# Row 0's attention maxima moved into the mixer's last stretch, and the late rows' norm and queries spread over rows 3 to 10

## The chip, the cores and the metric

One core of one Trainium2 chip. The metric is the device time of one execution in microseconds (us). The core has five engines with queues of their own, tied by semaphores: TensorE (PE in the profile, its weight loads PEld), VectorE (DVE), ScalarE (ACT), GpSimd (POOL) and SyncE (SP, which issues most transfers).

## The reference

Three layers, each added to its input and layer-normalised: a state-space mixer, a grouped-query attention over a given context, and a mixture of experts. The change touches the seam between the first two and the attention. The attention is:

```
x = layernorm(x + mixer(x));  x = layernorm(x + attention(x, ctx, ctx));  x = layernorm(x + experts(x))
attention(q, k, v): 32 query heads, 8 key heads of width 8, 16 rows of 128 tokens
    scores = q k^T / sqrt(8);  out = softmax(scores) v
```

## The kernel before

The kernel is two blocks, one after the other; every engine has a program of its own in each, and the second block starts when all engines have ended the first.

**The mixer** (`mixer`, from L84) runs 32 steps, a step for each of 8 head groups and 4 blocks of tokens (of 4 rows each). A step projects, takes scores of pairs of heads (`scores`, L822), weighs them by decays (`weigh`, L613, on VectorE), multiplies with the values (`outputs`, L833), adds the skip (`add_skip`, L625), gates (`gate_y`, L631), splits the result in a high half (`high_y`, L427, ScalarE) and a low half (`low_y`, L636, VectorE), and projects it out (`out_project`, L846) and adds it to the residual `acc` (`add_out`, L640, VectorE). The work of a step runs on into the next, so behind the last step stands a tail of these operations: VectorE's at L766 to L771, TensorE's at L936 to L942, ScalarE's at L547 to L550. When a block of 4 rows is finished it is normalised (`norm_part`), GpSimd splits each row's queries into 16-bit parts (`split_q`), TensorE turns them (`turn_q`, L898, through the one bank `pturn`) and ScalarE copies them to `q_rows` (`evac_q`, L448). That is done here for rows 0 to 11. Rows 12 to 15, the late rows, end with the last step and are normalised in the second block. The keys (`k_rows`) are loaded by SyncE during the last steps.

**The attention** (`attention_and_experts`, from L944) takes the 16 rows one by one. For the softmax each row b needs its maxima first: eight matmuls of queries on keys (`for_max`, L1534), eight VectorE reductions (`row_max`, L1334, into `mx`), a TensorE transpose (`turn_max`, L1571), ScalarE's negation into `neg_mx` (`negate_max`, L1223), and a SyncE transfer that writes the negated maxima as extra rows of `q_rows` (`store_max`, L1076). Then eight score matmuls (`shifted`, L1546) give scores less their maximum, ScalarE takes the exponentials (`exponential`, L1228), TensorE multiplies with the values (`times_values`, L1555, two halves), ScalarE copies (`evac_out`, L1234), TensorE turns the result (`turn_out`, L1563), VectorE inverts the sums and divides (`invert_sums`, `divide`, L1341 to L1350), and GpSimd adds to the residual (`add_heads`, L1123).

The order on each engine is written out by hand. TensorE's row b is the plan of L1593, in which F is a score matmul of row b, D a maximum matmul of row b + 2, X the transpose of the maxima of b + 1, A a value product, T a turn, and a quote means row b - 1:

```
plan = "F0 F1 D0 F2 A1' D1 X0 D2 F3 F4 F5 T1' D3 D4 A0 D5 F6 F7 D6 T0 D7".split()
```

VectorE's is L1356, with M a maximum of row b + 2, s an inversion and / a division:

```
plan = "/0' M0 M1 M2 s1' M3 M4 /1' M5 M6 M7 s0".split()
```

PSUM has eight banks. The maximum matmuls alternate between two (`pmax`), row 1's between four. The scores go round a ring of three (`ptr`), and a turned query takes a place in that ring (L976 to L981): before, behind the eighth score of rows 2 to 5. `ring_free` (L986) makes a matmul wait until the use three places earlier has been read, by the exponential or by VectorE's copy of a query (`evac_query`, L1329). Row 0 has all its maxima ahead of everything (L1585), then row 1's; VectorE takes the late rows' statistics right behind those (L1354) and normalises all four late rows behind row 0 (L1368 to L1370). GpSimd splits the late queries beside the residual additions of rows 0 to 3 and casts one expert weight each beside rows 4 to 6 (L1134 to L1142).

## Time and profile before

| | us |
|---|---|
| median of 3 runs (766.18 to 767.46) | 766.42 |
| the profiled execution, its own time | 771.25 |
| its span, first to last instruction | 769.4 |
| busy: PE / DVE / ACT / POOL | 734.7 / 578.6 / 451.4 / 385.4 |
| the seam between the blocks, near | 556 |
| attention's rows, up to about | 683 |

The span is from the first to the last instruction. Matmuls are pipelined, so a busy PE isn't one at its peak. In a timeline row stand the start, the length from the first start to the last end, the engine, the line, the operation, what it writes and reads, the count, and in brackets the idle time before it and what ended that. PEclk is the clock that TensorE was granted, 1.00 being 2.4 GHz and 0.50 1.2 GHz.

### The profile page before, as it was taken

The numbers are of one execution on the slowest core, as the hardware profiler recorded it, in microseconds if no ns is written. First come the engines' busy times: TensorE is split into PE (matmuls) and PEld (weight loads), VectorE is DVE, ScalarE is ACT, GpSimd is POOL, SyncE is SP. The second block draws the span as 40 slices with busy tenths as digits, with TensorE's granted clock in tenths as the row PEclk, the third lists the DMA queues.
The fourth block names the chain that finished last, engine by engine and source line by source line (L and its number), as shares of the span: only waits on it lengthen the run. The fifth ranks groups of instructions, "written<-read, shape, count | busy, mean of one in ns | idle before, by whom it ended". The sixth has DMA issues, their size and how long they took to land. (4 is left out here: it accounts for less than half of the span.)

```text
span 769.4 us, 17375 instructions
## 1 busy us (share of the span) xinstructions
PE 734.7 (95%) x5929; PEld 407.0 (53%) x5938; DVE 578.6 (75%) x1134; ACT 451.4 (59%) x885; POOL 385.4 (50%) x439
## 2 busy tenths in 40 slices
PE   8899999999999999999999999999689999989797
PEld 3456565555655556555565655556423444335464
DVE  5568768687676767858677688887588889986777
ACT  7735446654444764444476453555537788877576
POOL 2858427473362655435357783554303321359744
PEclk9999999999999999999999999999969999999999
DMA  6565433115522242631313323340032000000001
GB/s 204 175 198 175 94 55 55 63 48 107 175 56 55 55 98 49 156 94 55 82 45 90 85 70 76 70 90 13 10 128 83 19 23 23 23 1 2 29 29 56
DMA packets 34299, 57.92 MB, mean 75 GB/s; under 512 B 7056, under 2 KB 11920, under 8 KB 33680
## 3 DMA queue, kind: packets, MB, share of 16 engines
q1 hardware_dynamic: 33680, 57.08, 28.0%
q8 instruction: 23, 0.38, 0.2%
q10 hardware_dynamic: 576, 0.31, 0.1%
q14 instruction: 20, 0.16, 0.1%
HBM read 54.10 MB, written 2.36 MB: 73 GB/s over the span
## 5 line engine op out<-in xcount | busy, mean ns | idle before, releaser
L285 POOL TENSOR_TENSOR cum_rows<-cum_rows,cum_t 128x512 f32<-128x512 f32 x128 | 136.5, 1076 | 197.7 <-DMA cum_rows<-cum_scratch 197.7
L788 PE MATMUL pring<-xt_hi,w_hi 128*128 (+1 forms) x576 | 172.5, 381 | 0.0
L788 PE MATMUL pring<-xt_lo,w_hi 128*128 (+1 forms) x576 | 171.9, 380 | 0.0
L788 PE MATMUL pring<-xt_hi,w_lo 128*128 (+1 forms) x576 | 171.5, 379 | 0.0
L650 DVE TENSOR_TENSOR bt<-pring,bt 128x512 f16<-128x512 f32 x128 | 88.1, 688 | 73.4 <-ACT bt L442 73.3
L442 ACT CAST bt<-pring 128x512 f16<-128x512 f32 x128 | 74.6, 583 | 115.3 <-PE pring L788 115.2
L654 DVE TENSOR_TENSOR ct<-pring,ct 128x512 f16<-128x512 f32 x128 | 88.2, 689 | 54.5 <-ACT ct L446 54.2
L830 PEld LDWEIGHTS pscore<-ct,bt 128*128 128x128 f16 x1536 | 96.6, 98 | 34.4 <-issue 6.2
L830 PE MATMUL pscore<-ct,bt 128*128 128x128 f16 x1536 | 107.2, 220 | 3.8 <-issue 2.2
L446 ACT CAST ct<-pring 128x512 f16<-128x512 f32 x128 | 74.8, 585 | 52.4 <-PE pring L788 52.2
L1336 DVE TENSOR_REDUCE mx<-bank_at 128x4 f32<-128x512 f32 x128 | 83.5, 689 | 14.3 <-PE bank_at L1544 13.2
L788 PEld LDWEIGHTS pring<-xt_lo,w_hi 128*128 128x128 f16 x576 | 56.6, 98 | 68.6 <-issue 1.1
L788 PEld LDWEIGHTS pring<-xt_hi,w_lo 128*128 128x128 f16 x576 | 56.5, 98 | 68.3 <-issue 0.7
L622 DVE TENSOR_TENSOR mt<-pscore,cum_rows 128x512 f32<-128x512 f32 x128 | 87.0, 681 | 0.9 <-ACT cum_rows L436 0.9
L436 ACT ACTIVATE cum_rows<-cum_rows 128x512 f32<-128x512 f32 x128 | 81.0, 634 | 0.7 <-POOL cum_rows L296 0.7
L296 POOL TENSOR_SCALAR_AFFINE_SELECT cum_rows<-cum_rows 128x512 f32<-128x512 f32 x128 | 81.1, 645 | 0.0
L1232 ACT ACTIVATE probs<-bank_at 128x512 f32<-128x512 f32 x128 | 68.5, 599 | 14.2 <-PE bank_at L1553 12.6
L788 PEld LDWEIGHTS pring<-xt_hi,w_hi 128*128 128x128 f16 x576 | 50.7, 98 | 42.5 <-issue 7.8
L266 POOL TENSOR_TENSOR w_lo<-w_raw,w_hi 128x512 f16<-128x512 f32 x34 | 41.5, 1240 | 26.7 <-ACT w_raw L408 26.7
L1544 PE MATMUL bank_at<-k_rows,q_rows 128*128 128x512 f16 x128 | 48.8, 416 | 5.5 <-DVE mx L1336 3.9
L1126 POOL TENSOR_TENSOR acc<-acc,att 128x128 f32<-128x128 f32 (+1 forms) x32 | 15.0, 470 | 76.5 <-DVE att L1349 76.5
L1461 DVE SCALAR_TENSOR_TENSOR hid<-bank_at,weight,act_s 128x128 bf16<-128x128 f32 x128 | 35.9, 343 | 11.7 <-PE bank_at L1661 6.5
(157 smaller groups left out, 983.1 us busy)
## 6 DMA issues: line engine op xcount, KB each, us to landing
cum_rows<-cum_scratch SPq DMA_DIRECT2D x32, 1024.0 KB, 8.0
w_raw<-in_w_in SPq DMA_DIRECT2D x35, 256.0 KB, 6.8
q_rows<-in_xt SPq DMA_DIRECT2D x4, 512.0 KB, 11.0
acc<-in_x SPq DMA_DIRECT2D x1, 2048.0 KB, 7.9
vals<-in_vals SPq DMA_DIRECT2D x16, 128.0 KB, 2.0
out<-acc SPq DMA_DIRECT2D x7, 256.0 KB, 2.1
w_raw_e<-in_w_up SPq DMA_DIRECT2D x1, 1024.0 KB, 5.0
w_raw_e<-in_w_gate SPq DMA_DIRECT2D x1, 1024.0 KB, 7.0
```

Source lines behind the costliest of these rows:

```text
L285: nc.gpsimd.tensor_tensor(rows[:, par, :, q], rows[:, par, :, q], own, ALU.subtract).then_inc(sem("since"), 1)
L296: nc.gpsimd.affine_select(rows[:, par, :, q], rows[:, par, :, q], [[0, NB], [1, L]], ALU.is_ge, never, base=0, channel_multiplier=-1).then ...
L436: nc.scalar.activation(rows[:, par, :, e % 4], rows[:, par, :, e % 4], ACT.Exp).then_inc(sem("decay_exp"), 1)
L442: nc.scalar.copy(bt[:, s % 2, 0], bank[f"B{s}"][:]).then_inc(sem("b_hi"), 1)
L446: nc.scalar.copy(ct[:, s % 2, 0], bank[f"C{s}"][:]).then_inc(sem("c_hi"), 1)
L622: nc.vector.tensor_tensor(mt[:, par, s % 4].rearrange("p (b n) -> p b n", b=NB), pscore[(s + 1) % 2][:].rearrange("p (b n) -> p b n", b=NB ...
L650: nc.vector.tensor_tensor(bt[:, s % 2, 1], bank[f"B{s}"][:], bt[:, s % 2, 0], ALU.subtract).then_inc(sem("b_evac"), 1)
L654: nc.vector.tensor_tensor(ct[:, s % 2, 1], bank[f"C{s}"][:], ct[:, s % 2, 0], ALU.subtract).then_inc(sem("c_evac"), 1)
L788: mm = nc.tensor.matmul(bank[name][:], w[:, c, k, cols], x[:, k, bass.ds(n % TB, 1), :].rearrange("p o n -> p (o n)"), start=(i == 0), sto ...
L830: mm = nc.tensor.matmul(pscore[(s + 1) % 2][:, cols], bt[:, s % 2, pb, cols], ct[:, s % 2, pc, cols], start=(i == 0), stop=(i == 2))
L1232: nc.scalar.activation(probs[:, i], ring_bank("scores", 8 * b + i)[:], ACT.Exp, scale=float(8.0 ** -0.5)).then_inc(sem("probs"), 1)
L1336: nc.vector.tensor_reduce(mx[:, slot, :, i], banks[i % len(banks)][:].rearrange("p (k n) -> p k n", k=4), AX.X, ALU.max).then_inc(sem("max ...
```

## The change

Row 0's eight maximum matmuls and reductions, the transpose, the negation and the store are issued in the mixer's tail, in three banks free by then; the tiles `mx` and `neg_mx` and five semaphores are shared by both blocks. ScalarE's copies of queries 9, 10 and 11 stand in another order about the high half. In attention, row 0 has an order of its own: row 1's maxima in four banks (other ones than before) between row 0's scores, and row 2's maxima behind them. The late rows' statistics, aggregates and normalisations come in pairs or fours behind VectorE's rows 3 to 7 (`late_norm`). The late queries are turned in rows 7 to 10 and not behind rows 2 to 5, and in mid-row, behind the sixth score, with VectorE's copy behind its sixth maximum. GpSimd's splits move along, and its power for the late rows stands behind the third weight cast.

```diff
 mixer, SyncE, at the end
             sp.wait_ge(sem("k_load"), 16 * 28)
+            sp.wait_ge(sem("neg_max"), 1)
+            sp.dma_start(q_rows[96::8, 0:1].rearrange("p o t g n -> p (o t g n)"), neg_mx[:, 0]).then_inc(sem("max_row0"), 16)
 mixer, ScalarE, the tail
             evac_q(8)
+            evac_q(9)
             high_y(STEPS)
-            for b in range(9, BATCH - NB):
-                evac_q(b)
+            evac_q(10)
+            evac_q(11)
+            act.wait_ge(sem("mx_turn"), 1)
+            nc.scalar.mul(neg_mx[:, 0], mx_t, -1.0).then_inc(sem("neg_max"), 1)
 mixer, VectorE, the tail
             weigh(STEPS, -1)
+            row_max(0)
+            row_max(1)
             add_skip(STEPS)
             gate_y(STEPS)
+            row_max(2)
+            row_max(3)
             low_y(STEPS)
+            for i in range(4, 8):
+                row_max(i)
             add_out(STEPS, 0)
             add_out(STEPS, 1)
 mixer, TensorE, the tail (first_max = [pring[2], pring[3], pscore[1]], mx_t in pring[2])
+            def for_max(i):
+                if i == 0:
+                    pe.wait_ge(sem("b_evac"), 8 * STEPS + 1)
+                elif i == 1:
+                    pe.wait_ge(sem("c_evac"), 8 * STEPS + 2)
+                elif i == 2:
+                    pe.wait_ge(sem("mixed"), 8 * STEPS + 4)
+                else:
+                    pe.wait_ge(sem("max_red"), i - 2)
...
             scores(STEPS, -1)
+            pe.wait_ge(sem("k_load"), 16 * 28)
+            for i in range(3):
+                for_max(i)
             turn_q(8)
             outputs(STEPS - 1, 1)
             turn_q(9)
+            for_max(3)
+            for_max(4)
+            turn_q(10)
+            for_max(5)
+            for_max(6)
             out_project(STEPS, last=True)
-            turn_q(10)
+            for_max(7)
             turn_q(11)
+            pe.wait_ge(sem("max_red"), 8)
+            nc.tensor.transpose(mx_t, mx[:, 0].rearrange("p k i -> p (k i)"), ident[:]).then_inc(sem("mx_turn"), 1)
 attention, the ring and the banks
+        early_max = bank[0:2] + [pmx, pturn]
+        turns_at = 7
...
-            if 2 <= b < 2 + NB:
-                ring.append(("query", b - 2))
+            if 0 <= b - turns_at < NB:
+                ring.insert(len(ring) - 2, ("query", b - turns_at))
 attention, GpSimd
-            for i in range(NB):
-                add_heads(i, 0)
-                split_q(i)
-                add_heads(i, 1)
+            for b in range(3):
+                add_heads(b, 0)
+                add_heads(b, 1)
             for i, (name, w) in enumerate((("w_up", w_up), ("w_gate", w_gate), ("w_down", w_down))):
                 pool.wait_ge(sem(f"in_{name}"), 16)
                 nc.gpsimd.tensor_copy(w[:], w_raw[:, i]).then_inc(sem("w_bf16"), 1)
-                add_heads(NB + i, 0)
-                add_heads(NB + i, 1)
+                if i == 2:
+                    pool.wait_ge(sem("last_var"), 1)
+                    r = rstd[:, late:]
+                    nc.gpsimd.tensor_tensor(r, r, expo[:, 0:NB], ALU.pow).then_inc(sem("last_rstd"), 1)
+                add_heads(3 + i, 0)
+                add_heads(3 + i, 1)
             pool.wait_ge(sem("w_bf16"), 3)
+            split_q(0)
+            split_q(1)
+            for i in range(2, NB):
+                add_heads(turns_at - 3 + i, 0)
+                add_heads(turns_at - 3 + i, 1)
+                split_q(i)
 attention, ScalarE, row 0
-            negate_max(0, 0)
-            row(0, 0, first=True)
+            for i in range(6):
+                exponential(0, i)
+            evac_out(0, 0)
+            exponential(0, 6)
+            exponential(0, 7)
+            negate_max(1, 1)
 attention, VectorE
-            for i in range(8):
-                row_max(0, 0, i)
...
-                row_max(1, 1, i, banks=pmax + bank[4:6])
-            layer_norm_stats(nc, dve, sem, acc, stats, mean_var, rstd, "last", (TB - 1,))
-
-            plan = "/0' M0 M1 M2 s1' M3 M4 /1' M5 M6 M7 s0".split()
+                row_max(1, 1, i, banks=early_max)
+
+            plan = "/0' M0 M1 M2 s1' M3 M4 /1' M5 Q0 M6 M7 s0".split()
+
+            def late_norm(b):
+                if b in (3, 4):
+                    for i in range(2 * b - 6, 2 * b - 4):
+                        nc.vector.bn_stats(stats[:, i], acc[:, late + i]).then_inc(sem("last_stats"), 1)
+                elif b == 5:
+                    dve.wait_ge(sem("last_stats"), NB)
+                    for i in range(NB):
+                        nc.vector.bn_aggr(mean_var[:, late + i], stats[:, i]).then_inc(sem("last_aggr"), 1)
+                    dve.wait_ge(sem("last_aggr"), NB)
+                    nc.vector.tensor_scalar(rstd[:, late:], mean_var[:, late:, 1], EPS, None, ALU.add).then_inc(sem("last_var"), 1)
+                elif b in (6, 7):
+                    dve.wait_ge(sem("last_rstd"), 1)
+                    for i in range(2 * b - 12, 2 * b - 10):
+                        normalise_row(nc, acc, mean_var, rstd, late + i).then_inc(sem("last_x"), 1)
...
-            dve.wait_ge(sem("last_rstd"), 1)
-            for b in range(late, BATCH):
-                normalise_row(nc, acc, mean_var, rstd, b).then_inc(sem("last_x"), 1)
-            row(1, 1)
-            row(2, 0)
-            for i in range(NB):
-                evac_query(i)
-                row(3 + i, (3 + i) % 2)
-            for b in range(3 + NB, BATCH - 2):
+            for b in range(1, BATCH - 2):
                 row(b, b % 2)
+                late_norm(b)
 attention, TensorE
-            for i in range(8):
-                for_max(0, i, first=True)
-            turn_max(0, 0)
-            for i in range(8):
-                for_max(1, i, banks=pmax + bank[4:6])
...
-            plan = "F0 F1 D0 F2 A1' D1 X0 D2 F3 F4 F5 T1' D3 D4 A0 D5 F6 F7 D6 T0 D7".split()
+            plan = "F0 F1 D0 F2 A1' D1 X0 D2 F3 F4 F5 Q0 T1' D3 D4 A0 D5 F6 F7 D6 T0 D7".split()
...
-            row(0, 0, first=True)
+            for i in range(4):
+                for_max(1, i, banks=early_max)
+            for i in range(3):
+                shifted(0, 0, i)
+            for i in range(4, 8):
+                for_max(1, i, banks=early_max)
+                if i < 7:
+                    shifted(0, 0, i - 1)
+            times_values(0, 0, 0)
+            shifted(0, 0, 6)
+            shifted(0, 0, 7)
+            turn_max(1, 1)
+            turn_out(0, 0)
+            for i in range(8):
+                for_max(2, i)
             for b in range(1, BATCH - 2):
                 row(b, b % 2)
-                if 2 <= b < 2 + NB:
-                    turn_query(b - 2)
```

## Rows read from the trace of the kernel before

**Rows 1.** Windows: mixer tail, and attention in mid-course (busy us of each engine)

```profile
546.00:556.00 10.00, 4.16 (x68) 3.36 (x68) 4.34 (x6) 4.39 (x5) 2.81 (x4) 1.00 0.01 2
...
618.00:640.00 22.00, 22.00 (x137) 8.67 (x136) 20.15 (x41) 17.80 (x37) 4.87 (x8) 1.00 0.10 26
```

**Rows 2.** Timeline of the mixer's last stretch

```profile
547.76 0.75 DVE L628 SCALAR_TENSOR_TENSOR skip<-val_t,dskip,py 128x512 f32<-128x512 f32 x1 [1.21 <-PE py L842]
...
550.22 0.69 DVE L638 TENSOR_TENSOR y_parts<-skip,y_parts 128x512 f16<-128x512 f32 x1 [0.68 <-ACT y_parts L431]
...
551.98 1.35 DVE L645 TENSOR_TENSOR acc<-pring,acc 128x512 f32<-128x512 f32 x2 [1.07 <-PE pring L856]
...
554.81 1.01 ACT L450 COPY q_rows<-pturn 128x1024 f16<-128x1024 f16 x1 [0.79 <-PE pturn L905]
```

**Rows 3.** Timeline where attention starts

```profile
556.83 5.47 DVE L1336 TENSOR_REDUCE mx<-bank_at 128x4 f32<-128x512 f32 x8 [3.50 <-PE bank_at L1544]
...
563.08 6.56 SPq L1079 DMA_DIRECT2D q_rows<-neg_mx  x2
563.22 4.88 DVE L1336 TENSOR_REDUCE mx<-bank_at 128x4 f32<-128x512 f32 x8 [0.92 <-PE bank_at L1544]
...
566.16 0.92 PE L1553 MATMUL bank_at<-q_rows,k_rows 128*128 128x512 f16 x2
...
568.01 1.40 DVE L1790 BATCH_NORM_STATS2 stats<-acc 128x6 f32<-128x256 f32 x4
...
569.94 2.09 DVE L1336 TENSOR_REDUCE mx<-bank_at 128x4 f32<-128x512 f32 x3
...
575.99 0.59 PE L1553 MATMUL bank_at<-q_rows,k_rows 128*128 128x512 f16 x2
...
576.97 1.29 DVE L1760 TENSOR_SCALAR acc<-acc,mean_var,rstd 128x256 f32<-128x256 f32 x4
```

**Rows 4.** Windows of 1 us at the clock's fall and return

```profile
556.00:557.00 1.00, 0.62 (x2) 0.13 (x2) 0.17 (x1) 0.28 (x2) 0.00 (x0) 0.79 0.00 0
...
566.00:567.00 1.00, 1.00 (x3) 0.15 (x1) 1.00 (x3) 0.17 (x1) 0.00 (x0) 0.59 0.00 0
```

**Rows 5.** Timeline of row 7

```profile
620.76 0.59 PE L1553 MATMUL bank_at<-q_rows,k_rows 128*128 128x512 f16 x2
...
622.06 0.68 DVE L1336 TENSOR_REDUCE mx<-bank_at 128x4 f32<-128x512 f32 x1
...
623.27 0.81 PE L1553 MATMUL bank_at<-q_rows,k_rows 128*128 128x512 f16 x3
...
623.68 1.58 ACT L1232 ACTIVATE probs<-bank_at 128x512 f32<-128x512 f32 x3
...
624.88 1.07 PE L1560 MATMUL bank_at<-probs,vals 128*32 128x512 f32 x8
...
625.87 0.39 PE L1544 MATMUL bank_at<-k_rows,q_rows 128*128 128x512 f16 x1
...
626.30 1.99 DVE L1336 TENSOR_REDUCE mx<-bank_at 128x4 f32<-128x512 f32 x3
...
627.40 0.59 PE L1553 MATMUL bank_at<-q_rows,k_rows 128*128 128x512 f16 x2
```

**Rows 6.** The profile's page, DMA issues: size, and us to landing

```profile
vals<-in_vals SPq DMA_DIRECT2D x16, 128.0 KB, 2.0
```

**Rows 7.** Timeline: a pair of normalisations beside a query split, in the mixer

```profile
544.73 1.23 DVE L1760 TENSOR_SCALAR acc<-acc,mean_var,rstd  x2
```

**Rows 8.** Timeline of a query's turn and copy behind row 2

```profile
590.11 0.61 PE L1582 MATMUL bank_at<-ident,q_parts 128*128 128x128 f16 x8
...
590.56 0.59 PE L1553 MATMUL bank_at<-q_rows,k_rows 128*128 128x512 f16 x2
...
591.09 0.63 DVE L1332 COPY q_rows<-bank_at 128x1024 f16<-128x1024 f16 x1
...
591.77 0.39 PE L1553 MATMUL bank_at<-q_rows,k_rows 128*128 128x512 f16 x1 [0.40 <-DVE q_rows L1332]
```

More of the change, by code:

```diff
@@ L68, in build @@
                  "q_parts": sb("q_parts", [P, 2, 8, 4, 32], F16), "ident": sb("ident", [P, P], F32), "ident16": sb("ident16", [P, P], F16)}
-        mixer(nc, io, acc, moments, heads)
+        heads["mx"], heads["neg_mx"] = sb("mx", [P, 2, 4, 8], F32), sb("neg_mx", [32, 2, L], F16)
+        shared = {name: sem(name) for name in ("max_mm", "max_red", "mx_turn", "neg_max", "max_row0")}
+        mixer(nc, io, acc, moments, heads, shared)
         w_up, w_gate, w_down = (sb(n, [P, EXPERTS * 2 * P], BF16) for n in ("w_up", "w_gate", "w_down"))
@@ L81, in split_query, with mixer @@
     return nc.gpsimd.tensor_tensor(q_parts[:, slot, :, 1, :], x, q_parts[:, slot, :, 0, :], ALU.subtract)
-def mixer(nc, io, acc, moments, heads):
+def mixer(nc, io, acc, moments, heads, shared):
     with ExitStack() as ctx:
-        sb, ps, sem = makers(nc, ctx)
+        sb, ps, sem = makers(nc, ctx, shared)
         xt_hi = sb("xt_hi", [P, KT, TB, TOK], F16)
@@ L935, in _ @@
             step(STEPS - 1, range(4, 8))
+            def for_max(i):
[7 more added lines that the diff above has]
+                    pe.wait_ge(sem("max_red"), i - 2)
+                q = q_rows[:, 0:1, i // 4, i % 4, :].rearrange("p o n -> p (o n)")
+                k = k_rows[:, 0:1, i // 4].rearrange("p o k n -> p (o k n)")
+                nc.tensor.matmul(first_max[i % 3][:], q, k, start=True, stop=True).then_inc(sem("max_mm"), 1)
             scores(STEPS, -1)
+            pe.wait_ge(sem("k_load"), 16 * 28)
+            for i in range(3):
+                for_max(i)
             turn_q(8)
@@ L1236, in evac_out, with row @@
                 nc.scalar.copy(out_t[:, t], pout[:]).then_inc(sem("out_evac"), 1)
-            def row(b, slot, first=False, last=False):
+            def row(b, slot):
                 exponential(b, 0)
@@ L1241, in row @@
                 exponential(b, 2)
-                if not first:
-                    evac_out(b - 1, 1)
-                if not last:
-                    negate_max(b + 1, 1 - slot)
+                evac_out(b - 1, 1)
+                negate_max(b + 1, 1 - slot)
                 for i in range(3, 6):
@@ L1365, in row @@
                         row_max(b + 2, slot, n)
+                    elif what[0] == "Q":
+                        if 0 <= b - turns_at < NB:
+                            evac_query(b - turns_at)
                     elif not (first and what.endswith("'")):
@@ L1532, in rows, with for_max @@
                 return t[:, bass.ds(b, 1)].rearrange("p o t g n -> p (o t g n)")
-            def for_max(b, i, first=False, banks=pmax):
+            def for_max(b, i, banks=pmax):
                 t, g = i // 4, i % 4
@@ L1583, in turn_query, with row @@
                 mm.then_inc(sem("q_turn_mm"), 1)
-            for i in range(8):
-                for_max(0, i, first=True)
-            turn_max(0, 0)
-            for i in range(8):
-                for_max(1, i, banks=pmax + bank[4:6])
-            plan = "F0 F1 D0 F2 A1' D1 X0 D2 F3 F4 F5 T1' D3 D4 A0 D5 F6 F7 D6 T0 D7".split()
-            def row(b, slot, first=False):
+            plan = "F0 F1 D0 F2 A1' D1 X0 D2 F3 F4 F5 Q0 T1' D3 D4 A0 D5 F6 F7 D6 T0 D7".split()
+            def row(b, slot):
                 for what in plan:
                     n, before = int(what[1]), what.endswith("'")
-                    if first and before:
-                        continue
                     if what[0] == "F":
@@ L1605, in row @@
                         turn_max(b + 1, 1 - slot)
+                    elif what[0] == "Q":
+                        if 0 <= b - turns_at < NB:
+                            turn_query(b - turns_at)
                     elif what[0] == "A":
```

27 lines of the change are left out of this document (13 added, 14 removed).

## The prediction

> **What bounds the kernel now.** I read the windows first: they show TensorE all but full in the middle of attention and less than half full in the mixer's last 10 us [rows 1]. Then I read the timeline at the seam of the two blocks, where the change works. The mixer's last stretch [rows 2] is one serial chain: VectorE waits 1.21 us for the output matmul, adds the skip, gates, writes the low part, adds the result to the residual, and ScalarE copies the last query until 555.82 (554.81 + 1.01). Attention then starts cold [rows 3]: VectorE takes eight maxima of row 0, then the maxima of row 1, then the late rows' statistics, and row 1's first score matmuls start at 575.99. TensorE's granted clock meanwhile falls in the 557th us to 0.50, that is 1.2 of 2.4 GHz, and returns in the 567th [rows 4]; a score matmul steps at 0.215 at full clock (0.81 for three against 0.59 for two, [rows 5]) and so at 0.43 at half. From row 7 on [rows 5] a row lasts 627.40 - 620.76 = 6.64 us and TensorE never waits, so an added TensorE instruction costs its whole length and an added VectorE one only what exceeds its slack. That slack: maximum 0 of a row ends at 622.06 + 0.68 = 622.74; the maximum matmul that waits for it goes out one step before the three scores, at 623.27 - 0.22 = 623.05. With 0.04 for the semaphore the slack is 0.27 us.
>
> **The seam.** Eight score matmuls and eight maxima come into the mixer's tail, with a transpose, a negation and an 8 KB store. TensorE's part is 8 x 0.215 and lies in its gaps. On VectorE, idle 5.66 us of the ten [rows 1], two maxima go from 546.55 to about 547.85 at a step of 0.65 (1.99 for three, [rows 5]), so the skip moves from 547.76 to 547.85. Maxima 2 and 3 run while ScalarE casts the high part, which ended before the low part's start at 550.22. They end at 550.85, so the low part slips 0.6 us to 550.85. The output projection slips with it. Maxima 4 to 7 then take 551.5 to 554.1 (0.65 a step), and the two additions (1.35) end at 555.4 where they ended at 553.33: that is inside the 555.82 at which ScalarE ended. ScalarE's queue: query 8 and 9 now ahead of the high part, 10 right behind it, 11 when its turn has passed maximum 7's matmul, about 553.7 to 554.75. Then it negates a 32-partition tile, some 0.3, to 555.05. Behind it SyncE issues the store, in about 0.7 us by a share of the two merged in [rows 3], to 555.75. All these ends lie below 555.82, so I take the block's end as unmoved, bounds -0.3 and +1.0. Removed for it: row 0's eight maxima, transpose and negation in the new block, from 556.83 to 563.22 = 6.39 us [rows 3].
>
> **The store's landing.** Row 0's scores wait for it. From above: in [rows 3] the same store is issued at 563.08 and the first score matmul starts at 566.16, so it takes at most 3.1 us. From below: 2.0, the median of the 128 KB value loads [rows 6]. From 555.05 that is 557.05 to 558.15. I take 558.0, near the upper row as it is the same transfer. Row 0's scores then go out at 558.0.
>
> **Row 0 and row 1's start.** I assume the clock again falls near 556.8, since TensorE has as little to do between 554 and 556.4 as before, and returns about 563.5, because TensorE now has work without a break from 558.0 on. Four matmuls of row 1's maxima go out by 557.4 into four banks, three scores at 558.0 to 559.3, then seven alternating matmuls (four for maxima 4 to 7, three scores) at 0.43 each to 562.3. The last maximum matmul, out at 561.85, ends at 562.45 (0.38 at full clock, some 0.6 at half) and its maximum at 563.2. The value product takes 0.99 at full clock (624.88 to 625.87, [rows 5]) and 2.0 at half; 1.2 us of it lie before 563.5, so it ends at 563.9. Two scores take 0.43, the transpose of maxima and the output's about 0.6 (a row's 6.64 less sixteen steps of 0.215 and two products leaves 1.2 for twice that), and a ScalarE copy of some 0.6 must end between product and output transposes: that brings TensorE to 565.15. Row 2's maxima start at 565.55, two banks, 0.65 a step. The eighth matmul needs the sixth maximum, done at 565.55 + 5 x 0.65 + 0.69 = 569.5, and row 1's first scores stand right behind: 569.6 against 575.99, **-6.4 us**. That it equals the 6.39 removed is chance: the statistics (568.01 to 569.94, 1.9 us) leave this stretch too, but row 2's maxima, which lay beside row 0's exponentials, now follow them. Row 1 starts with VectorE 0.38 us behind its steady place, a wait of 0.23. Row 1's own store, behind its negation at 566.0, lands by 569.1 at most, just in time.
>
> **The norm, spread.** It is added behind VectorE's rows 3 to 7. A pair of statistics is 2 x 0.35 (1.40 for four [rows 3]), less the slack 0.27: 0.43, twice. Aggregates and variance: 569.94 - 569.41 = 0.53, less 0.27: 0.26. A pair of normalisations, 2 x 0.32 (1.29 for four, row 576.97), less 0.27: 0.37; the second pair meets a query's delay, 0.50. GpSimd's power runs a row ahead of its use, covered; it also casts each expert weight as now and no one waits for those. Sum **+2.0**. The normalisations now run while GpSimd splits queries: a pair took 1.23 us beside such a split in the mixer [rows 7], so each may cost 0.6 more. I take none, as the split can't start before the first of the pair is done; upper bound +1.2. By the Trainium skill, page "GPSIMD Engine Reference", section Specifications, GpSimd shares VectorE's SBUF interfaces and contends with its two-port instructions; by that rule the pairs stretch and the whole sum would be 763.5.
>
> **The queries, mid-row.** Now a query costs 0.45 on TensorE (590.11, next scores 590.56) and the third score behind it, due 0.65 later at 591.21, starts at 591.77 as it waits for VectorE's copy, 0.56 [rows 8]: 1.01 each. After the change the query stands behind the sixth score and takes the bank of the fourth. Its exponential starts at 623.68 [rows 5] and lasts 0.59 (three take 1.58, each starting about 0.1 ahead of the last one's end), to 624.27; TensorE is ready at 623.27 + 0.65 = 623.92: a wait of 0.40 with the semaphore. The turn, 0.45. All behind it moves by 0.85: the matmul at 625.87 goes out at 626.72, its maximum 5 at 627.14; the copy follows 0.66 later and takes 0.63, to 628.43. The next row's first score needs that bank and would start at 628.25: 0.23 more. Maximum 6, behind the copy, ends at 629.03, but the next row's first maximum matmul would go out at 628.91 and needs its bank: 0.16. Sum 0.40 + 0.45 + 0.23 + 0.16 = 1.24 each, **0.9 us more for four than now**.
>
> **The sum.** From row 1's first score to row 7's, before: 620.76 - 575.99 = 44.77 = 6 x 6.64 + 4.93 (four queries 4.04, normalisation 0.89). After, over rows 1 to 11: 0.23 + 2.0 + 4 x 1.24 = 7.2. So -6.4 + 7.2 - 4.93 = **-4.1 us**. The profiled execution took 771.25 (span 769.4), 4.8 above the median 766.42; I carry the difference over: 766.4 - 4.1 = **762.3**. TensorE bounds what follows row 11, so it shifts whole.
>
> **The rivals.**
> - The clock doesn't fall at the seam, or returns by 560, as TensorE has work in the gaps that it had before: then row 1 starts at 567.6 (store at 558.0, four-bank maxima to 561.9, product to 561.8, maxima of row 2 from 563.4). Result 760.3. Chance 0.15.
> - The clock stays low through row 0, to 567 as now [rows 4]: the product takes 2.0, all behind it goes at half pace, row 1 starts at 571.4, result 764.1. For: it stayed low 10 us in before. Against: there TensorE idled between maxima. Chance 0.15. The Trainium skill, page "TensorE: Matmul & The Clock Gate", section "Part 1: The HAM clock gate", has throttling as the default that only sustained activity lifts; by that rule the low case costs what this one does, and 762.3 would become 764.1.
> - The block's close waits for the store to land: attention starts 1.2 to 2.3 us later, 763.5 to 764.6. No row shows a transfer outstanding at a close. Chance 0.12.
> - The mid-row query is covered, only its 0.45 stays, as the exponential or copy comes sooner: 4 x 0.79 less, 759.1. Chance 0.06.
> - The change doesn't shorten the seam: maxima push the mixer's end by what they save. VectorE would need its 5.66 us of idle elsewhere; within 0.2% of before. Chance 0.05.
> - Slower: the clock stays down into the rows. At half clock a TensorE-bound row loses half of each us. To 571.4 it costs 1.8, then 0.5 per us: the gain is gone at 576, and at 580 the result is 768.4. Chance 0.04.
>
> The forecast itself has 0.43. **Range**: the clock cases, the late close and the contention bound give 759.9 to 765.0; outside stand the last two and most of the covered query, with the tail's own clock phases. Differences within 0.2% (1.5 us) can't be told from none: faster 0.87, same 0.08, slower 0.05.
>
> **What would show it.** Right: attention's first maximum near 556.8, row 1's first score near 569.6; a row of 6.64 without late work, about 7.1 for rows 3 and 4, near 7.9 with a query, its turn waiting for ScalarE's exponential and the next row's first score for VectorE's copy. Wrong: that maximum later than 557.8, a granted clock of 0.5 beyond 565, normalisation pairs over 1 us, or query rows at 7.1.

## The result, and the profile after

| | before | after |
|---|---|---|
| median, us (lowest to highest) | 766.83 (766.18 to 767.46, 4 runs) | 760.16 (759.59 to 760.83, 4 runs) |
| ratio, 95% interval | | 0.9904 (0.9879 to 0.9929) |
| profiled execution: its time, its span | 771.25, 769.4 | 760.83, 759.0 |
| last step's skip product starts (`add_skip`) | 547.76 | 542.90 |
| from there to attention's first maximum | 9.07 | 9.42 |
| first maximum to row 1's mark | 21.34 | 12.97 |
| row 1's mark to row 14's mark | 90.81 | 94.06 |
| row 14's mark to the end | 100.42 | 99.65 |

The mark of a row is the transpose of maxima (X) in its stretch of TensorE's order. The change made the kernel faster, by 6.7 us of the medians where the forecast had 4.1; its range, 759.9 to 765.0, holds the 760.16, but as a gain on its own starting value (1.4 to 6.5) it just misses the 6.7. The mixer ahead of the seam varies between executions of one kernel (the skip product starts at 547.76 and 543.36 in two profiles of the kernel before, but is followed by 221.64 and 221.44 us), so I compare profiles from the last step's skip product on, and medians second. From there to the end is **221.64 before and 216.10 after: -5.5 us**.

Not all of that is the change's. Of the 5.5, 0.8 stand behind row 14's mark, where the change touches nothing. That last part takes 100.3 to 100.5 us in the nine profiles of this document in which TensorE's clock is low for 3.4 us somewhere between 718 and 734 us (before among them, 730.7 to 734.1), and 99.5 to 99.7 in the five in which it isn't (after among them). From the skip product to row 14's mark the gain is 121.2 - 116.5 = 4.8 us, and 121.0 - 116.6 = 4.4 in the second profiles of both kernels. The start of the mixer varies with the clock too: in four profiles it is low for 3.4 us once or twice between 26 and 45 us, and three of these have the skip product at 546.07 to 547.76 (before, after again, norm left out), the fourth and the ten others at 542.5 to 544.2.

The seam in the timeline of the kernel after, which answers to [rows 2] and [rows 3]:

```profile
542.90 0.75 DVE L638 SCALAR_TENSOR_TENSOR skip<-val_t,dskip,py 128x512 f32<-128x512 f32 x1
...
545.80 0.67 DVE L648 TENSOR_TENSOR y_parts<-skip,y_parts 128x512 f16<-128x512 f32 x1
...
548.95 1.28 DVE L655 TENSOR_TENSOR acc<-pring,acc 128x512 f32<-128x512 f32 x2
...
549.70 0.26 ACT L560 ACTIVATE neg_mx<-pring 32x128 f16<-32x128 f32 x1
550.05 0.71 SPq L265 DMA_DIRECT2D q_rows<-neg_mx  x1
...
552.32 2.49 DVE L1386 TENSOR_REDUCE mx<-bank_at 128x4 f32<-128x512 f32 x4 [2.09 <-PE bank_at L1599]
...
553.36 1.49 PE L1608 MATMUL bank_at<-q_rows,k_rows 128*128 128x512 f16 x3
...
563.11 0.59 PE L1608 MATMUL bank_at<-q_rows,k_rows 128*128 128x512 f16 x2
```

Row 0's first scores go out 1.04 us behind the first maximum, where row 0 before had all its maxima ahead of them, and row 1's first scores 10.79 behind it (before 575.99 - 556.83 = 19.16, forecast 569.6 - 556.8 = 12.8). Most of the difference to the forecast stands in the clock. Windows of 1 us of the same stretch (us, then PE, PEld, DVE, ACT, POOL busy, the granted clock, DMA share, GB/s):

```profile
551.00:552.00 1.00, 0.30 (x1) 0.14 (x2) 0.00 (x0) 0.28 (x2) 0.00 (x0) 0.76 0.04 8
552.00:553.00 1.00, 1.00 (x4) 0.37 (x3) 0.68 (x2) 0.00 (x0) 0.00 (x0) 0.50 0.39 129
...
554.00:555.00 1.00, 1.00 (x3) 0.27 (x2) 0.81 (x2) 0.97 (x3) 0.00 (x0) 0.53 0.00 0
555.00:556.00 1.00, 1.00 (x6) 0.49 (x5) 0.80 (x2) 1.00 (x4) 0.00 (x0) 1.00 0.00 0
```

TensorE is at its lower level, 1.2 of 2.4 GHz, for 3.4 us here, from 551.5 to 554.9. Before it was so for 13.7 us, in two stretches, of which [rows 4] show the ends of the first. It fell in a stretch of 2.3 us without a matmul, and rose when TensorE had worked without a break since 551.70.

Behind row 1 there is a wait that before did not have. The chain of waits of the kernel after, around row 2 (start, us, what):

```profile
565.97 0.08 SPq L1123
566.05 0.04 issue
566.09 5.21 DMA q_rows<-neg_mx
571.30 0.05 issue
571.35 0.61 PE bank_at L1608 x2
```

The 8 KB store of row 2's negated maxima takes 5.21 us from issue to landing. SyncE's part of the timeline shows what it stands behind:

```profile
559.25 0.68 SPq L1123 DMA_DIRECT2D q_rows<-neg_mx  x1
559.98 0.45 SPq L1129 DMA_DIRECT2D w_raw_e<-in_w_up  x1
560.46 0.43 SPq L1129 DMA_DIRECT2D w_raw_e<-in_w_gate  x1
560.94 0.43 SPq L1129 DMA_DIRECT2D w_raw_e<-in_w_down  x1
...
563.71 0.46 SPq L1131 DMA_DIRECT2D s_down<-in_s_down  x1
566.09 0.68 SPq L1123 DMA_DIRECT2D q_rows<-neg_mx  x1
```

The feed-forward weights, three loads of 1 MB and five small ones, are issued behind row 1's store, as before, but row 2's store now follows that one by 6.8 us and the last load by 2.4 (before by 10.0 and 5.5). TensorE waited 1.44 us for it:

```profile
571.35 0.61 PE L1608 MATMUL bank_at<-q_rows,k_rows 128*128 128x512 f16 x2 [1.44 <-DMA q_rows<-neg_mx]
```

From row 1's mark to row 14's the distances are 8.25, 6.64, 6.70, 6.86, 6.87, 6.71, 8.22, 8.28, 8.03, 8.02, 6.64, 6.64 and 6.20 us: the wait is in the first, the norm in the small excesses up to row 7, the queries in the four over 8.

### The profile page after: what moved, and what is told of

It reads as the page before. It is cut to its first block and busy times, and to the rows that moved or that the text cites. A ratio compares the mean times of both kernels' runs of the same rounds, so it can differ in the third digit from the quotient of the medians.

```text
span 759.0 us, 17379 instructions
## 1 busy us (share of the span) xinstructions
PE 729.5 (96%) x5938; PEld 403.8 (53%) x5938; DVE 575.7 (76%) x1134; ACT 450.5 (59%) x885; POOL 386.1 (51%) x439
## 5 line engine op out<-in xcount | busy, mean ns | idle before, releaser
L1386 DVE TENSOR_REDUCE mx<-bank_at 128x4 f32<-128x512 f32 x120 | 77.8, 687 | 9.1 <-PE bank_at L1599 8.0
L1280 ACT ACTIVATE probs<-bank_at 128x512 f32<-128x512 f32 x128 | 67.9, 600 | 14.4 <-PE bank_at L1608 13.7
L1599 PE MATMUL bank_at<-k_rows,q_rows 128*128 128x512 f16 x120 | 43.7, 392 | 4.2 <-PEq L88 2.3
L1351 ACT ACTIVATE act_s<-bank_at,weight 128x128 f32<-128x128 f32 x128 | 36.8, 374 | 12.5 <-PE bank_at L1721 8.0
```

The source lines that it names most:

```text
L1280: nc.scalar.activation(probs[:, i], ring_bank("scores", 8 * b + i)[:], ACT.Exp, scale=float(8.0 ** -0.5)).then_inc(sem("probs"), 1)
L1386: nc.vector.tensor_reduce(mx[:, slot, :, i], banks[i % len(banks)][:].rearrange("p (k n) -> p k n", k=4), AX.X, ALU.max).then_inc(sem("max ...
```

## The experiments

Each row of the table is one profile, and the median of the runs beside it; "low" is the time at 1.2 GHz from 14 us ahead of the first maximum to 26 us behind it, the other columns are distances in us. "Row 1's transpose of maxima" in the expectations is row 1's mark here.

| kernel | median | ratio (95%) | low | skip product to first maximum | to row 1's mark | to row 14's mark | skip product to end |
|---|---|---|---|---|---|---|---|
| before | 766.83 | | 13.7 | 9.07 | 21.34 | 90.81 | 221.64 |
| before again | 767.78 | 1.000 (0.9975 to 1.0026) | 17.1 | 10.12 | 20.08 | 90.84 | 221.44 |
| before, filled | 765.29 | 0.9977 (0.9955 to 0.9998) | 3.4 | 8.94 | 20.47 | 90.81 | 220.66 |
| after | 760.16 | 0.9904 (0.9879 to 0.9929) | 3.4 | 9.42 | 12.97 | 94.06 | 216.10 |
| after again | 761.02 | 0.9916 (0.9893 to 0.9940) | 6.8 | 9.21 | 14.91 | 92.51 | 217.04 |
| weights spread | 761.07 | 0.9904 (0.9871 to 0.9938) | 3.4 | 9.42 | 13.07 | 92.46 | 215.35 |
| query at row's end | 760.46 | 0.9910 (0.9878 to 0.9942) | 0 | 9.21 | 12.14 | 92.80 | 214.55 |
| norm left out | 761.28 | 0.9912 (0.9880 to 0.9944) | 0 | 9.21 | 12.14 | 93.04 | 214.73 |
| seam filled | 761.18 | 0.9917 (0.9885 to 0.9950) | 3.4 | 9.21 | 13.56 | 92.50 | 215.59 |
| seam alone | 759.23 | 0.9895 (0.9866 to 0.9924) | 6.8 | 9.22 | 14.92 | 89.99 | 213.81 |
| weights and query | 758.71 | 0.9877 (0.9848 to 0.9905) | 3.4 | 9.42 | 12.81 | 91.36 | 213.19 |
| weights and query again | 759.95 | 0.9896 (0.9870 to 0.9923) | 3.4 | 9.41 | 12.77 | 91.36 | 213.99 |
| these and lulls filled | 758.78 | 0.9891 (0.9860 to 0.9921) | 0 | 9.21 | 12.13 | 91.35 | 212.19 |
| seam alone, weights, lulls | 757.49 | 0.9872 (0.9844 to 0.9900) | 0 | 9.21 | 12.87 | 90.82 | 212.49 |

What is missing to the last column is row 14's mark to the end, 99.5 to 99.7 or 100.3 to 100.5, and which of the two it is differs between executions of one kernel (99.6 and 100.5 for the weights and query) with the low stretch near 720 us, as said above. So of a difference in the last column 0.8 can be chance; the sum of the three columns before it is free of that. In the first runs of weights and query one of six executions took 1517.38 us, the others 757.38 to 760.74 (their median is 758.26); why isn't known.

The medians of kernels near each other say little here. The intervals of the ratio are 0.3% to either side, 2.5 us, and three single edits that were expected 1.0 to 1.6 us under the changed kernel (weights, query, norm) came out at 760.46 to 761.28, none under 760.16. What follows rests on the profiles, one for each run.

**The kernel before, word for word.**

> The kernel before, unchanged, for a second trace. Theory N: the 4.86 us by which the mixer's tail came earlier in the profile of after (skip at 542.90 against 547.76) are not the change's, and the profiled execution of before was just a slow one. Then this profile has the skip of the last step near 543.3 and a span near 765. Rival: the change shortens the mixer. Then the skip is again near 547.8 here, whatever the median.

The theory holds: the skip product is at 543.36 and the span 764.8. The sum from there to the end repeats to 0.2 us, but its parts don't. The clock was low in one stretch, from 5.5 us ahead of the first maximum to 11.5 behind it, so the mixer's tail took 1.05 more and the way to row 1's mark 1.26 less, as the first profile's second low stretch (13.4 to 16.8 us behind the first maximum) is missing.

**The weights' loads spread** behind the stores of rows 2 to 5:

```diff
-            for i, w in enumerate(("w_up", "w_gate", "w_down")):
-                sp.dma_start(w_raw[:, i], io[w]).then_inc(sem(f"in_{w}"), 16)
...
+            for i, w in enumerate(("w_up", "w_gate", "w_down")):
+                supply(2 + i, i % 2)
+                sp.dma_start(w_raw[:, i], io[w]).then_inc(sem(f"in_{w}"), 16)
+            supply(5, 1)
```

> After, with the three expert weights' loads issued one behind each of the stores of rows 2, 3 and 4, and the small tensors behind row 5's, in place of all behind row 1's store. Theory: in after row 2's store (issued 566.09, landed 571.30) queued behind the weights' 3.5 MB and TensorE waited 1.4 us for it. Here the wait is gone, the transposes of maxima of rows 1 and 2 stand 6.64 apart and not 8.25, and the time is 1.6 us below after, 758.6. Rival: the store is late of itself, or another store is held up in turn: within 0.5 us of after.

The distance from row 1's mark to row 2's is 6.64 instead of 8.25, all others are those of the changed kernel: the wait was 1.6 us and the loads made it. The median, 761.07 for an expected 758.6, did not show it.

**The query turned at the row's end**, as before, in the late rows 7 to 10:

```diff
-                ring.insert(len(ring) - 2, ("query", b - turns_at))
+                ring.append(("query", b - turns_at))
...
-            plan = "F0 F1 D0 F2 A1' D1 X0 D2 F3 F4 F5 Q0 T1' D3 D4 A0 D5 F6 F7 D6 T0 D7".split()
+            plan = "F0 F1 D0 F2 A1' D1 X0 D2 F3 F4 F5 T1' D3 D4 A0 D5 F6 F7 D6 T0 D7".split()
```

> After, with the late queries turned behind rows 7 to 10 and copied by VectorE ahead of the next row's plan, as before the change placed them, the rows left as after has them. Theory: mid-row a query costs 1.38 us (rows 8.03 long against 6.64), at the row's end 1.02 as in before. Time 1.4 us below after, 758.7, and rows with a query 7.66 long. Rival (the change's design): the mid-row place is the cheaper one, and this is no faster or up to 1 us slower.

Rows 7 to 10 take 8.47 and three times 7.66, together 31.45 instead of 32.55: 1.1 us less, where 1.4 was expected. Turned in mid-row a query costs more than at the end. In mid-row the forecast's two larger waits are there; TensorE in the kernel after, at the first turn and at the next row's first score:

```profile
609.00 0.61 PE L1637 MATMUL bank_at<-ident,q_parts 128*128 128x128 f16 x8 [0.35 <-ACT probs L1280]
...
613.27 0.59 PE L1608 MATMUL bank_at<-q_rows,k_rows 128*128 128x512 f16 x2 [0.17 <-DVE q_rows L1382]
```

**The late norm left out.** Statistics, power and normalisation of rows 12 to 15 are not computed.

> After without the late rows' statistics, aggregates, power and normalisation: rows 12 to 15 enter attention unnormalised. Theory from the trace of after: they cost 1.0 us in rows 3 to 8 (0.06, 0.22, 0.23, 0.07, 0.20, 0.26), so 759.1. The prediction on record had 2.0, so 758.1. A third: all of it is hidden or falls where TensorE has slack, 760.1.

Rows 3 to 6 take 26.62 for 27.14, and rows 7 to 10 take 32.10 for 32.55: the spread norm costs 0.97 us. VectorE around the place of a pair of statistics, in this run and then in the kernel after, where they stand:

```profile
600.87 0.25 DVE L1388 RECIPROCAL rsum<-bank_at 128x16 f32<-128x16 f32 x1
601.15 0.29 DVE L1393 TENSOR_TENSOR att<-bank_at,rsum 128x128 f32<-128x128 f32 x1
```

```profile
592.37 0.24 DVE L1392 RECIPROCAL rsum<-bank_at 128x16 f32<-128x16 f32 x1
592.54 0.69 DVE L1408 BATCH_NORM_STATS2 stats<-acc 128x6 f32<-128x256 f32 x2
593.14 0.27 DVE L1397 TENSOR_TENSOR att<-bank_at,rsum 128x128 f32<-128x128 f32 x1
```

From the inversion's start to the division's it is 0.28 without and 0.77 with them: 0.69 us of work delay VectorE by 0.49. The query rows without norm, 8.03, 8.02, 8.03, 8.02, give a query as (32.10 - 4 x 6.64) / 4 = 1.38.

**The seam filled.** Six matmuls into a bank that nobody reads, behind the mixer's transpose of maxima.

```diff
+            for i in range(6):
+                nc.tensor.matmul(py[:], ident16[:], k_rows[:, 0:1, 0].rearrange("p o k n -> p (o k n)"), start=True, stop=True)
```

> The changed kernel with six matmuls more on TensorE behind the mixer's transpose of the maxima, into a bank that nobody reads. Theory (the clock costs what its low stretch is long: 3.4 us low in the changed kernel's profile, none in the runs with the query at the row's end and without the norm): with TensorE occupied in the seam the clock stays at 2.4 GHz, first maximum to row 1's transpose of maxima takes 12.1 to 12.3 us instead of 12.97, the last step's skip product to the end about 1 us less than 216.10, some 215.0, median about 760. Rival (what TensorE does in the seam doesn't decide it): a low stretch of 3 us or more is there again. Second rival (the six delay the block's close): skip product to first maximum over 9.6 instead of 9.42.

Theory and rival were both half right. The clock did not fall in the seam, and the first maximum and row 0's mark came as in the two profiles without a low stretch (4.94 apart), but it fell 9.3 us behind the first maximum, after a second lull, in which TensorE does no more than keep pace with VectorE's maxima of row 2. Windows of the run with the seam filled:

```profile
551.00:552.00 1.00, 0.28 (x2) 0.00 (x0) 0.00 (x0) 0.00 (x0) 0.00 (x0) 1.00 0.00 0
...
559.00:560.00 1.00, 0.39 (x1) 0.10 (x1) 1.00 (x3) 0.00 (x0) 0.00 (x0) 1.00 0.02 4
...
561.00:562.00 1.00, 0.58 (x3) 0.19 (x2) 1.00 (x3) 0.00 (x0) 0.00 (x0) 1.00 0.85 328
562.00:563.00 1.00, 0.84 (x3) 0.33 (x3) 1.00 (x2) 0.00 (x0) 0.00 (x0) 0.53 0.96 401
```

There it met row 1's scores and product and cost 13.56 - 12.14 = 1.4 us, more than in the seam. And row 2's distance fell to 6.67: what the low clock took, the wait for the store gave back, since the store was asked for later. Rows 0 and 1 together ended where they do without a low stretch (20.23 from the first maximum to row 2's mark, and 20.22 with the query at the row's end).

**The kernel before, filled**: 18 such matmuls in its mixer's tail, and one behind each of row 0's eight maximum matmuls.

> The kernel before with matmuls more on TensorE, into banks that nobody reads: 18 in the mixer's last stretch, and one behind each maximum matmul of attention's row 0. Nothing else is changed, so the long wait for row 0's maxima stays. Theory (the low clock of before, 13.65 and 17.06 us in its two profiles, comes from TensorE's thin work around the seam, and about a quarter of it is time lost): the low stretch shrinks under 4 us, first maximum to row 1's transpose takes 17.5 to 19 us instead of 21.34 and 20.08, the last step's skip product to the end some 219 instead of 221.64 and 221.44; median 2 us under the kernel before. Rival (the clock falls whatever TensorE does there, or its fall costs nothing): low stretch of over 10 us, or the same 20 to 21 us from first maximum to row 1's transpose, ratio 1.000.

The low time shrank as expected, and the median is 2.1 us under that of the kernel before on the same chip, 767.39. But the stretch to the end fell by 0.9 us only, to 220.66, where 219 was expected, and row 1's mark came no sooner than in the kernel before again, 20.47 for 20.08. The windows show where the 3.4 us stood:

```profile
563.00:564.00 1.00, 0.00 (x0) 0.00 (x0) 0.96 (x6) 0.19 (x2) 0.00 (x0) 1.00 0.00 0
564.00:565.00 1.00, 0.08 (x1) 0.08 (x2) 0.97 (x4) 0.00 (x0) 0.67 (x1) 0.77 0.11 16
565.00:566.00 1.00, 1.00 (x3) 0.35 (x4) 0.90 (x2) 0.01 (x1) 0.34 (x1) 0.50 0.82 123
566.00:567.00 1.00, 1.00 (x3) 0.30 (x2) 0.26 (x1) 1.00 (x3) 0.00 (x0) 0.50 1.10 467
```

TensorE idled while VectorE took the statistics, the clock fell, and row 0's scores met it. From row 0's mark to row 1's this run took 9.84 us; the kernel before again, whose 17.1 us had ended 11.5 us behind the first maximum, took 8.32, and the kernel before's first profile, with its low stretch of 3.4 us in nearly the same place, 9.79. So 3.4 us under dense work cost 1.5, while 17.1 us under VectorE's maxima cost about 1.1 there (first maximum to row 0's mark 11.76 against 10.63) and about 1 more in the mixer's tail (10.12 against 9.07). So the length of a low stretch alone doesn't give its cost; what TensorE has to do in it counts.

**The seam alone**: early maxima and row 0's order as in the change; statistics in one piece behind row 1's maxima, normalisations in one piece, queries in rows 2 to 5, all as before.

```diff
-            plan = "/0' M0 M1 M2 s1' M3 M4 /1' M5 Q0 M6 M7 s0".split()
+            plan = "/0' M0 M1 M2 s1' M3 M4 /1' M5 M6 M7 s0".split()
...
+            layer_norm_stats(nc, dve, sem, acc, stats, mean_var, rstd, "last", (TB - 1,))
...
+            for b in range(late, BATCH):
+                normalise_row(nc, acc, mean_var, rstd, b).then_inc(sem("last_x"), 1)
```

> The changed kernel with its early maxima and row 0's order, but late norm, query splits and query turns where the kernel before had them (statistics and normalisation in row 0 in one piece, queries in rows 2 to 5 at the row's end). Theory (VectorE waits in row 0 for the keys' scores and exponentials anyway, so that the statistics and the four normalisations cost less there than spread): row 0 longer by 1.3 us, norm -1.0 and queries -1.4 in the later rows, the wait for row 2's stored maxima -0.8: skip product to the end about 214.2 instead of 216.10, median 758.5 to 760. Rival (spreading is needed: in one piece they hold up row 0's exponentials and row 1's maxima): row 0 longer by over 4 us, slower than the changed kernel by 1 us or more.

The stretch to the end met its number, 213.81, but not by its sum: the clock was low for 6.8 us, and row 0 was 1.95 longer. The changed kernel's second profile has nearly the same low stretches and so is its mate: 14.91 against 14.92 to row 1's mark. VectorE in the two, first the changed kernel again, then the seam alone:

```profile
563.11 4.91 DVE L1386 TENSOR_REDUCE mx<-bank_at 128x4 f32<-128x512 f32 x8 [1.95 <-PE bank_at L1599]
```

```profile
551.71 5.19 DVE L1381 TENSOR_REDUCE mx<-bank_at 128x4 f32<-128x512 f32 x8 [1.88 <-PE bank_at L1599]
556.80 1.40 DVE L1849 BATCH_NORM_STATS2 stats<-acc 128x6 f32<-128x256 f32 x4
...
558.85 4.94 DVE L1381 TENSOR_REDUCE mx<-bank_at 128x4 f32<-128x512 f32 x8
```

Row 2's maxima start 7.14 us behind the first maximum in both (563.11 - 555.97, 558.85 - 551.71): the 2 us of statistics stand wholly in the 1.95 in which VectorE waits for row 2's first matmul. In one piece they were free here, with the clock low around row 0's scores; spread, they are part of a cost of 0.97.

**Weights and query together**, run twice:

> The changed kernel with two repairs together: the feed-forward weights' loads spread behind rows 2 to 5's stores, and the queries turned at the row's end. Theory (the two losses add: 1.6 us waited for row 2's stored maxima, 1.4 for the four queries within rows): periods of rows 2 and 9 to 12 as 6.64 and 7.7 to 8.5 us, skip product to the end 213.0 to 214.5 instead of 216.10, median about 758, under both kernels. Rival (the run with the weights spread measured 761.07, so the wait was covered by something): skip product to the end not under 215, median 760 or more.

> The kernel with weights and queries repaired once more, word for word, beside the changed kernel on one chip. Theory (it saves 1.6 + 1.4 us in the chain of waits): 2 to 3 us under the changed kernel's median, ratio to the kernel before 0.987 to 0.989, skip product to the end 212.5 to 214.3. Rival (the 758.71 was the luck of one job): within 1 us of the changed kernel.

From row 1's mark to row 14's 91.36 us both times against 94.06, so the two losses add: 1.6 + 1.1. By the medians it is 1.1 us under the changed kernel on the same chip, less than the 2 to 3 expected; by the stretch to the end 3.0, 213.99 against 217.04, with their last parts alike.

**The changed kernel again.**

> The changed kernel once more, word for word, as the mate of the two others on this chip. Theory: median 760 to 761, ratio 0.990 to 0.992; skip product to the end 215.5 to 217; row 2's wait for its stored maxima (period of row 2 8.0 us or more where the others have 6.64) and the four query rows at 8.0 to 8.3 are there again, whereas the stretches of low clock may lie elsewhere. Rival (the wait for row 2's maxima was one execution's chance): period of row 2 under 7.

The query rows and the median repeated. Row 2's wait did not: its distance is 6.69. The rival holds for that run, and the run shows why. Its clock was low for 6.8 us, its row 1 had its mark 1.94 later, and the store landed in time. The low clock and the store's wait cover each other: to row 2's mark it is 21.60 us in one profile and 21.22 in the other.

**Both lulls filled**: weights and query, the six matmuls in the seam, and one behind each of the first seven maximum matmuls of row 2.

> The kernel with weights and queries repaired (758.71 in the last job, skip product to the end 213.19, clock low for 3.4 us around the first maximum), with TensorE's two lulls filled by matmuls into banks that nobody reads: six in the seam, as in the run with the seam filled, and one behind each of the first seven of row 2's maximum matmuls, where that run's low stretch stood instead. Theory (each low stretch follows a stretch in which TensorE does little, and 3.4 us of it cost about 1): no low stretch up to row 12, first maximum to row 1's transpose of maxima 12.1 to 12.3 us instead of 12.81, and row 2's 6.6 behind it, skip product to the end 212 to 212.7, median about 758. Rival (the low stretch moves on once more to another lull, or the seven delay row 2's maxima): a low stretch of 3.4 us elsewhere, skip product to the end 213 or more.

As expected: no low stretch, 12.13 us, then 6.64. That agrees with the clock falling behind lulls and with fillers holding it, and so does the next run, the only other one with both lulls filled. It is no proof: two of the eight profiles of the changed kernel and its versions without fillers (query at the row's end, norm left out) have no low stretch there either, and they have the same 2.3 us without a matmul ahead of the new block.

**Seam alone, weights, lulls.**

> The run with the seam alone (213.81 from the last step's skip product to the end, 6.8 us of low clock), with two edits of other runs added: the feed-forward weights' loads spread behind rows 2 to 5's stores, and TensorE's two lulls filled. Late norm and queries stay where the kernel before had them. Theory (the late rows' statistics in one piece stand in VectorE's wait and cost nothing or up to 0.6 us, where the spread norm costs 1.0): no low stretch, first maximum to row 1's transpose of maxima 12.1 to 12.8 us, row 2's 6.64 behind it, skip product to the end 211.0 to 212.3, the least of all kernels here, median 757 to 758.5. Rival (with the full clock the wait in row 0 is only 1.46 us long and the statistics' 2.05 push row 2's maxima, and the weights' loads or fillers delay more): first maximum to row 1's transpose 13.2 or more, skip product to the end 212.5 or more, no better than spread.

Between the two theories. The lowest median of all, 757.49, but 212.49 to the end, no better than spread. At the full clock VectorE's wait is shorter, the statistics push row 2's maxima by 0.7, and the four normalisations at once push the maxima that stand in row 1's order, those of row 3; TensorE waits for them:

```profile
563.90 1.29 DVE L1825 TENSOR_SCALAR acc<-acc,mean_var,rstd 128x256 f32<-128x256 f32 x4
...
566.04 0.39 PE L1603 MATMUL bank_at<-k_rows,q_rows 128*128 128x512 f16 x1 [0.69 <-DVE mx L1385]
```

So in one piece the norm costs 12.87 - 12.13 = 0.7 in row 0 and 7.50 - 6.64 = 0.9 in row 1, 1.6 us against 0.97 spread, once the clock stays up. By the intervals of their medians the two last versions can't be told apart, nor from the changed kernel. From the skip product to row 14's mark both gain 8.3 to 8.5 us on the kernel before's first profile, the change itself 4.8 and 4.6 in its two.

## Why the prediction was right and wrong

- **The mixer's tail, right.** Skip, low part, additions, negation and store came in the forecast's order; the tail lost 0.35 us from the skip product to the first maximum, inside the bounds of -0.3 to +1.0. The close itself took longer: SyncE's issue ended at 550.76 and its next one, the new block's first, started at 551.51, 0.75 later; before, ScalarE's copy ended at 555.82 and SyncE's first issue followed at 556.09, 0.27 later; 0.75 is the same in all eleven runs with the early store, and what it is made of isn't shown. It is not the store's landing, the rival's case: behind 551.51 packets of the store still moved, as these windows show (the loads issued at 551.51 bring nothing before 552.4).

```profile
551.25:551.51 0.26, 0.00 (x0) 0.00 (x0) 0.00 (x0) 0.00 (x0) 0.00 (x0) 1.00 0.10 24
551.51:552.00 0.49, 0.30 (x1) 0.14 (x2) 0.00 (x0) 0.28 (x2) 0.00 (x0) 0.51 0.02 4
```

- **The store's landing, put too late, at no cost.** It was given up to 3.1 us; by its packets, the last of which fall before 552.0, it took under 2, from its issue at 550.05. Row 0's first scores follow the fourth maximum matmul without a wait.
- **The clock's return, wrong, and the step that failed.** "The clock again falls near 556.8 and returns about 563.5", 6.7 us behind the first maximum. It rose 2.6 us behind it (554.94). The forecast had an uninterrupted TensorE only from row 0's first score on and judged by the 10 us of [rows 4], in which TensorE had idled between maxima. The rival "returns by 560" gave row 1's first scores at 567.6, 10.8 us behind the first maximum, and 760.3; measured were 10.79 and 760.16. That the second number fits so well is luck, for it contains the later terms, of which the norm's, the queries' and a missing wait were off by 1.0, 0.6 and 1.6. The rival had a chance of 0.15 and should have had more: the row at which before's clock rose stood under a different load. And the place of the low clock is a matter of the execution: in the second profile of the changed kernel it was low from 0.8 to 4.3 and again from 11.1 to 14.5 us behind the first maximum, and row 1's mark came 1.9 later. The Trainium skill, page "TensorE: Matmul & The Clock Gate", section "Part 1: The HAM clock gate", which has the lower level as the default that sustained activity lifts, has that much in common with the runs here: the clock rose while TensorE worked without a break, and the two runs with both lulls filled have no low stretch. That the clock would stay low through row 0, for 764.1, was the prediction's own reading of it, not the page's, and did not come.
- **Row 0 and row 1's start, -6.4, became -8.4.** The forecast's sum and the rival's (10.8 us) differ by 2.0, and by the clock alone: six of the seven alternating matmuls and the value product ran at full pace. This is worked out; no run has the clock low for as long as the forecast had it. Inside the 10.8 two small errors cancel: row 2's maxima began 0.2 later than the rival had them and went at 0.60 a step (4.87 for eight) instead of 0.65. Without any low stretch row 1's mark comes another 0.8 earlier (12.14 for 12.97).
- **Norm, +2.0, measured +1.0.** By the distances with and without norm the pairs of statistics cost 0.22 and 0.23 for 0.43 each, the aggregates 0.07 for 0.26, and the pairs of normalisations 0.19 and 0.26 for 0.37 and 0.50. The slack of 0.27 was right, what was mis-sized is the length ahead of it: the forecast took the steps' own 0.70, 0.53 and 0.64, but between inversion and division they delay VectorE by 0.49, 0.31 and 0.44 (0.77, 0.59 and 0.72 with them for 0.28 without). Less 0.27 that is 0.22, 0.04 and 0.17. The normalisation pairs took 0.64 each (606.11 and 614.40), and GpSimd's splits started only at 606.57 and 614.78, in their last 0.2 to 0.3 us, so the +1.2 for contention did not come, and a full overlap wasn't tried.
- **The query in mid-row, 1.24, measured 1.38**, and its terms are the named ones. Beside a row without a query, in the kernel after, TensorE's way from three scores to the next turn is 1.16 - 0.64 = 0.52 longer (607.84 to 609.00, 640.20 to 640.84; forecast 0.40), the turn takes 0.44 (0.45), from there to the next row's first score it is 3.83 - 3.49 = 0.34 longer (613.27, 644.33; forecast 0.23), and to that row's first maximum matmul 0.51 - 0.43 = 0.08 (613.78, 644.76; forecast 0.16): 1.38 together. That it is dearer than at the row's end (1.02) came as forecast.
- **Not foreseen: the store's wait, 1.6 us.** "Row 1's own store lands just in time" was asked of row 1 alone. Row 2's store moved to 2.4 us behind the last of the weights' loads, which the change left in place. In the sum it was set off by two terms that came out smaller, the norm's and the last part's, and the last part's is chance.
- **The sum.** By the steps: seam +0.35 - 8.37, row 1's mark to the end +2.48 (forecast +2.27: norm -1.0, queries +0.6, wait +1.6, start lag -0.2, the last part of the kernel -0.8) = -5.5 for -4.1. Without the last part it is -4.8, and -4.4 in the second profiles, so in the stretch that it treated the forecast's total came close, by errors that cancel. The medians say -6.7 and, for the second pair on its own chip, -6.1. The 1.3 to 2.3 us between these and the profiles lie ahead of the skip product, behind row 14's mark or in executions that weren't profiled; profiles of one kernel differ in the first by up to 4.4 and in the second by 0.8 us, but where the difference comes from stays open.

## What to carry to other kernels

When work is moved out of a stretch, list the transfers that keep their place: a small store that comes closer behind large loads on the same queue can become the new wait. A slow clock cost more or less here by what the engine had to do in it, so ask which instructions will stand there, not only how long it lasted before. Ahead of taking a difference between two profiles for the change's, take each kernel's profile twice and look at the parts that the change doesn't touch. And a piece of work that is to be spread should first be held against the waits that it could stand in whole.

## What the runs showed of the hardware

- An 8 KB store issued (566.09) 2.4 us behind the last of eight loads (3.5 MB by their sizes) took 5.21 us to land, with the DMA engines at a share of about 1; with the loads spread the wait for it was gone.
- TensorE's clock fell in different places in executions of one kernel: 3.4 us around the first maximum in one, twice 3.4 us behind it in another. 3.4 us cost about 1.0 around the first maximum (0.8 behind it, 0.2 ahead) and 1.4 to 1.9 under scores and products (8.62 and 9.09 from row 0's mark to row 1's for 7.20 without, 9.79 for 8.32 in the kernel before).
- A low stretch of 3.4 us between 718 and 734 us goes with 0.8 us more behind row 14's mark, in nine of fourteen profiles, whatever the kernel.
- Two losses next to each other need not add: with a second low stretch the changed kernel's row 1 came 1.9 us later, but the store's wait vanished, and only 0.4 us was lost by row 2's mark.
